# Moving two additions per chunk of a feed-forward block to GpSimd, and one rounding to VectorE

## The chip, the cores and the metric

The kernel runs on one core of a Trainium2 chip. The metric is the device time of one execution in microseconds. The kernel before was timed three times: 3913.15 us in the median, 3912.57 to 3914.15.

## The reference

The input `x` holds 16 images of 24 channels and 56 by 56 pixels in float32. It goes through four layers. Each layer is a mixer (attention in windows, a state-space scan, a four-direction scan, a row LSTM) and then a feed-forward block, both with a residual addition:

```
x = x + mixer(_ln_c(x))              # normalised over the 24 channels
t = _to_tokens(x)
t = t + ffn(_ln_t(t), W1, b1, W2, b2)
x = _from_tokens(t, x)

def ffn(x, W1, b1, W2, b2):          # q_mul rounds to 5 exponent and 2 mantissa bits, q_acc to 5 and 10
    h = relu(_qlinear(x, W1, b1))    # 24 -> 96
    return _qlinear(h, W2, b2)       # 96 -> 24
```

`_qlinear(x, W, b)` is `q_acc(q_acc(q_mul(x) @ q_mul(W).T) + q_mul(b))`. The first format is held as float8 (e5m2), the second as float16.

## The kernel before

`x` lies in SBUF through the whole program as 128 lanes by 4 times 3136 columns: four groups of images at lanes 0, 32, 64 and 96 with 24 lanes each. A mixer writes its result to `mixed` in DRAM, and `feed_forward_phase` follows it, four times in all (layer 0 to 3). That function is what the change touches.

It cuts the 12544 columns into 32 chunks of N = 392. For chunk c it does this:

- SyncE loads the mixer's result of the chunk into one of four buffers (`load`, L220, four transfers, one for each lane group), up to six chunks ahead.
- `add_mixed`: VectorE adds it to `x` (L308).
- `subtract_mean`: TensorE multiplies the chunk by a centring matrix in float32 (L418) into the PSUM bank `xc_ff`.
- `square` (ScalarE, L362), `variance` (TensorE, L425, a product with an averaging matrix), then Ln and Exp on ScalarE (L368, L372), which give the inverse deviation.
- `quantize`: VectorE multiplies the centred bank by it and rounds to float8 (L285).
- `hidden_units`: TensorE makes the 96 hidden units of the four groups in two halves (L436). ScalarE rounds each half to float16 (`round_hidden`, L379), VectorE adds the bias and rectifies (`rectify`, L292), and then rounds all to float8 (`quantize_hidden`, L303).
- `second_product`: TensorE, four products into the bank `ps_y` (L449).
- `round_result`: ScalarE rounds that to float16 (L386). `add_bias` (L321) and `update` (L314) on VectorE add the bias and then the sum to `x`.
- In the layers 0 to 2 the updated chunk is normalised for the next mixer: `subtract_mean` into the bank `xc_ln`, square, `variance` into `ps_y`, Ln, Exp, and `norm` on VectorE (L330), which SyncE stores (L237). In the last layer SyncE stores the chunk of `x` itself (L231).

The chunks are pipelined by an order that is written out by hand. The function `slots` calls a body `slot(s)` on each engine for s = 0 to 34. In slot s an engine works on chunk s+1 (the centring for it), s (inverse deviation, `quantize`), s-1 (hidden units), s-2 (second product, result) and s-3 (norm). The order within slot s is:

- VectorE: `quantize(s)`, `add_mixed(s+1)`, first half of `rectify(s-1)`, `add_bias(s-2)`, `update(s-2)`, second half of `rectify(s-1)`, `quantize_hidden(s-1)`, `norm(s-3)`.
- ScalarE: Ln and Exp of s, first half of `round_hidden(s-1)`, `round_result(s-2)`, the square for the norm of s-3, second half of `round_hidden(s-1)`, square of s+1, Ln and Exp for the norm.
- TensorE: both halves of `hidden_units(s-1)`, `second_product(s-2)`, centring for the norm of s-3, centring of s+1, variance for the norm, variance of s+1.

Every engine runs its instructions in the order written, and semaphores count the finished ones (`added`, `centred`, `quantized`, `biased`, `updated` and so on). GpSimd has no work in this function.

Of the kernel before, what the change touches and what calls it, by code (L numbers as in the profile page):

```python
# [12 lines left out]
ALU = mybir.AluOpType  # L13
# [112 lines left out]
AHEAD = 6  # L126


def feed_forward_phase(nc, x, mixed_dram, normed_dram, out_dram, w, st, layer, by_image=False):
# [6 lines left out]
    with ExitStack() as ctx:  # L136
# [37 lines left out]
        ff, ln = st.ff, st.ln  # L174

        all_loads = (layer + 1) * 6 * 16
        preps = 12
# [24 lines left out]
        with nc.Block() as block:  # L202
            @block.sync
            def _(sp):

                sp.dma_start(centre[:], w["centre"]).then_inc(st.weights_in, 16)
                sp.dma_start(average[:], w["average"]).then_inc(st.weights_in, 16)
                sp.dma_start(w1f[:], w["ff_w1"][layer]).then_inc(st.weights_in, 16)
                sp.dma_start(w2f[:], w["ff_w2"][layer]).then_inc(st.weights_in, 16)
                sp.dma_start(b1f[:], w["ff_b1"][layer]).then_inc(st.weights_in, 16)  # L210
                sp.dma_start(b2f[:], w["ff_b2"][layer]).then_inc(st.weights_in, 16)

                def load(j, k, b):
# [3 lines left out]
                    for g in range(G):  # L217
                        rows = (mixed_dram[j + g * J, :, k * N:(k + 1) * N] if by_image
                                else mixed_dram[c + g * CHUNKS])
                        sp.dma_start(group_rows(mixed[b], g), rows  # L220
                                     ).then_inc(st.mixed_in[b], 16)

# [18 lines left out]
                sp.wait_ge(st.prepared, prep0 + 1)  # L241
                for k in range(AHEAD):
# [14 lines left out]
            def _(dve):  # L257

                for b in range(UNROLL):
# [14 lines left out]
                dve.wait_ge(st.prepared, prep0 + 11)  # L274
# [4 lines left out]
                def quantize(c):  # L279
# [5 lines left out]
                    dve.tensor_tensor(xq[:], xc["ff"][:, 0:N], rstd["ff"][:], ALU.mult,  # L285
# [19 lines left out]
                def add_mixed(c, turn, u):  # L305

                    dve.wait_ge(st.mixed_in[u], (turn + (layer * (CHUNKS // UNROLL) + 1)) * G * 16)
                    dve.tensor_tensor(x[:, bass.ds(c * N, N)], x[:, bass.ds(c * N, N)],  # L308
                                      mixed[u][:], ALU.add).then_inc(ff["added"], 1)

                def update(c):

                    dve.wait_ge(ff["biased"], c + 1 + fb)
                    dve.tensor_tensor(x[:, bass.ds(c * N, N)], x[:, bass.ds(c * N, N)],  # L314
                                       yb[:], ALU.add).then_inc(ff["updated"], 1)
# [36 lines left out]
                add_mixed(0, 0, 0)  # L352
                slots(dve, slot)

            @block.scalar
            def _(act):
# [3 lines left out]
                def square(s, name, base, c):  # L360
                    act.wait_ge(s["centred"], c + 1 + base)
                    act.activation(squares[name][:], xc[name][:, 0:N], ACT.Square  # L362
# [19 lines left out]
                def round_result(c):  # L382

                    act.wait_ge(ff["summed"], c + 1 + fb)
                    reached(act, ff["biased"], c + fb)
                    act.activation(y16[:], ps_y[:, 0:N], ACT.Copy).then_inc(ff["summed16"], 1)  # L386

                def slot(s, turn, u, on):
# [4 lines left out]
                    if on[2]:  # L393
                        round_result(s - 2)
                    if not last and on[3]:
                        square(ln, "ln", nb, s - 3)
                    if on[1]:
                        round_hidden(s - 1, 1)
                    if has_next(s):
                        square(ff, "ff", fb, s + 1)  # L400
# [3 lines left out]
                square(ff, "ff", fb, 0)  # L404
# [4 lines left out]
            def _(pe):  # L409
                pe.wait_ge(st.weights_in, all_loads)  # L410
# [1934 lines left out]
```

## Time and profile before

| quantity | value |
|---|---|
| median of three runs | 3913.15 us |
| the profiled execution | 3912.36 us |
| its span in the trace | 3910.5 us |
| TensorE busy | 3205.9 us, 82% |
| VectorE busy | 2733.1 us, 70% |
| ScalarE busy | 2623.9 us, 67% |
| GpSimd busy | 1638.0 us, 42% |
| mean granted TensorE clock | 0.943 of full speed |

The busy times are sums over the whole program, and the four feed-forward stages are four stretches in it, which begin at 822.8, 2391.5, 3134.5 and 3719.5 us of the trace; the last ends with the program. GpSimd has no instruction in these stretches. The granted clock says what share of full speed (2.4 GHz) TensorE had; it is either 1 or 0.5 at any moment, and a number between is a mean.

### The profile page before, as it was taken

Reading aid. Unit: us, or ns where it says so; the run is one execution under the profiler, and the core shown is the slowest. Engines: PE = TensorE matmul, PEld = TensorE weight load, DVE = VectorE, ACT = ScalarE, POOL = GpSimd, SP = SyncE. Lnnn points to the kernel's source line nnn. Section 1 sums busy time; section 2 is a strip of 40 time slices with the busy share of each in tenths; the row PEclk is TensorE's granted clock in tenths of the full one; section 3 lists DMA queues with packets and bytes.
Section 4 is the critical chain, followed back from the end, with each engine's and each line's share of the span. In section 5 each row is a group of like instructions: output and inputs, shape, how many; then the busy total and the mean of one; then the engine's idle time right before and its main releaser. Section 6 shows DMA issues by size and latency. Waiting matters only on the chain. (4 is left out here: it accounts for less than half of the span.)

```text
span 3910.5 us, 70731 instructions
## 1 busy us (share of the span) xinstructions
PE 3205.9 (82%) x20680; PEld 1815.2 (46%) x20680; DVE 2733.1 (70%) x4347; ACT 2623.9 (67%) x4852; POOL 1638.0 (42%) x1502
## 2 busy tenths in 40 slices
PE   5799999978678898999999666878888678677666
PEld 2688888844224343444444222433343334566522
DVE  2566666657319998999999992749999867122256
ACT  4455555559698888989889434966666378465556
POOL 0233333310147888989889761007677600000000
PEclk9899999989889999999999997989999889798988
DMA  4100000012365747576674522210000022400022
GB/s 95 28 14 14 14 14 14 14 32 60 86 165 161 193 134 197 141 209 172 175 204 120 135 58 68 59 36 20 21 21 20 12 50 54 87 13 13 17 56 51
DMA packets 209512, 297.93 MB, mean 76 GB/s; under 512 B 73866, under 2 KB 193854, under 8 KB 208962
## 3 DMA queue, kind: packets, MB, share of 16 engines
q1 hardware_dynamic: 198546, 285.75, 28.2%
q10 hardware_dynamic: 10800, 10.34, 1.1%
q8 instruction: 58, 0.95, 0.1%
q14 instruction: 108, 0.88, 0.1%
HBM read 193.87 MB, written 102.03 MB: 76 GB/s over the span
## 5 line engine op out<-in xcount | busy, mean ns | idle before, releaser
L1586 POOL TENSOR_TENSOR mam_hc<-mam_h,mam_cs 128x896 f32<-128x896 f32 x336 | 704.0, 2096 | 181.4 <-DVE mam_h L1551 93.3
L1551 DVE TENSOR_TENSOR_SCAN mam_h<-mam_a,mam_kept,mam_dbx 128x448 f32<-128x448 f32 x672 | 737.5, 1127 | 19.9 <-ACT mam_a L1437 18.5
L1318 PE MATMUL mam_ps_y<-mam_hc,mam_ident 128*128 128x448 f32 x1344 | 569.7, 557 | 132.5 <-POOL mam_hc L1586 132.2
L1987 POOL TENSOR_TENSOR scan_ch<-scan_h,scan_cs 128x392 f32<-128x392 f32 x256 | 342.6, 1357 | 394.4 <-DVE scan_h L1931 317.3
L1437 ACT ACTIVATE mam_a<-mam_ft,mam_a_neg 128x448 f32<-128x448 f32 x672 | 409.3, 657 | 79.5 <-DVE mam_h L1551 78.7
L1318 PEld LDWEIGHTS mam_ps_y<-mam_hc,mam_ident 128*128 128x128 f32 x1344 | 248.5, 192 | 431.8 <-POOL mam_hc L1586 222.7
L1538 DVE TENSOR_TENSOR mam_dbx<-mam_ps_u,mam_bs 128x448 f32<-128x448 f32 x672 | 380.8, 610 | 34.2 <-DMA mam_bs<-dram_bc 34.2
L766 POOL TENSOR_TENSOR att_prob<-att_prob,att_share 128x588 f32<-128x588 f32 x128 | 151.6, 1184 | 452.5 <-DVE att_share L951 452.5
L2107 PE MATMUL lstm_ps<-lstm_hs,lstm_w_h 64*128 64x224 f32 x1344 | 175.8, 417 | 97.0 <-DVE lstm_hs L2190 97.0
L418 PE MATMUL f_xc_ff<-all_x,f_centre 128*128 (+1 forms) x256 | 127.8, 583 | 138.8 <-DVE all_x L308 138.7
L886 ACT ACTIVATE att_pt<-att_ps_t 128x512 f32<-128x512 f32 x128 | 76.4, 597 | 210.2 <-PE att_ps_t L827 210.2
L379 ACT ACTIVATE f_h<-f_hid 96x784 f16<-96x784 f32 x256 | 206.8, 810 | 0.0
L1819 PE MATMUL scan_ps_merged<-scan_ch,scan_w_merge 64*128 64x392 f32 x1024 | 202.6, 530 | 3.9 <-POOL scan_ch L1987 3.5
L2107 PEld LDWEIGHTS lstm_ps<-lstm_hs,lstm_w_h 64*128 64x128 f32 x1344 | 149.1, 222 | 120.9 <-DVE lstm_hs L2190 116.3
L867 ACT ACTIVATE att_keys<-att_ps_keys 24x392 f32<-24x392 f32 x384 | 186.5, 486 | 22.4 <-PE att_ps_keys L795 19.4
L1807 PE MATMUL scan_ps_in<-scan_xin,scan_w_in 128*128 128x392 f32 x512 | 187.5, 510 | 6.8 <-ACT scan_rest L1880 4.9
L837 PE MATMUL att_ps_out<-att_pt,att_vals 128*24 128x49 f32 x2048 | 189.5, 208 | 2.1 <-ACT att_pt L886 2.1
L839 PE MATMUL att_ps_out<-att_pt,att_vals 128*24 128x49 f32 x2048 | 187.3, 207 | 0.0
L803 PEld LDWEIGHTS att_ps_vals<-att_nvals,att_xw 128*64 128x64 f32 x4096 | 130.5, 138 | 75.5 <-issue 75.5
L2177 DVE TENSOR_TENSOR lstm_added<-lstm_gates,lstm_new 128x224 f32<-128x224 f32 x56 | 21.9, 392 | 204.7 <-ACT lstm_gates L2137 204.7
L957 DVE TENSOR_SCALAR att_result<-att_ps_out,att_b_out 24x392 f32<-24x392 f32 x128 | 78.6, 614 | 116.4 <-PE att_ps_out L839 116.4
L1931 DVE TENSOR_TENSOR_SCAN scan_h<-scan_decay_by_column,scan_h,scan_drive_by_column 128x392 f32<-128x392 f32 x112 | 158.8, 1418 | 0.2
(214 smaller groups left out, 7464.4 us busy)
## 6 DMA issues: line engine op xcount, KB each, us to landing
mam_taps<-normed SPq DMA_DIRECT2D x1008, 43.5 KB
mam_bs<-dram_bc SPq DMA_DIRECT2D x28, 896.0 KB, 14.3
mam_cs<-dram_bc SPq DMA_DIRECT2D x28, 896.0 KB, 16.6
mam_ft<-dram_steps SPq DMA_DIRECT2D x42, 448.0 KB, 4.8
normed<-f_staged SPq DMA_DIRECT2D x384, 38.1 KB
f_mixed<-mixed SPq DMA_DIRECT2D x384, 36.8 KB
dram_gs<-mam_gs SPq DMA_DIRECT2D x56, 224.0 KB, 2.1
mam_gt<-dram_gs SPq DMA_DIRECT2D x56, 224.0 KB, 2.7
```

What stands on the lines that cost most here:

```text
L379: act.activation(h16[:, 2 * a:2 * a + 2, :], hid[a][0:HID, :, 0:N], ACT.Copy).then_inc(ff["hidden16"], 1)
L837: pe.matmul(ps_out[0:C, cols], vals[p][:, win, 0:C], pt[p][:, q, 64 * half:64 * half + T], start=True, stop=False)
L839: mm = pe.matmul(ps_out[0:C, cols], vals[p][:, win, C:2 * C], pt2[p][:, q, 64 * half:64 * half + T], start=False, stop=True)
L1318: mm = pe.matmul(ps_y[p % 2][:, 0:MT], ident[:], hc[t % 2][:, i, :], start=False, stop=(t % 8 == 7 and i == 1))
L1437: act.activation(a[t % 3][:, i, :], ft[p % 2][:, 0, :], ACT.Exp, scale=a_neg[:, at:at + 1]).then_inc(decays, 1)
L1538: dve.tensor_tensor(dbx[:, i, 0:MT], ps_u[:, 0:MT], bs[:, 2 * pair + i, :], ALU.mult).then_inc(driven, 1)
L1551: dve.tensor_tensor_scan(h[:, n % 8, :], a[t % 3][:, i, :], dbx[:, i, 0:MT], kept[:, at:at + 1], ALU.mult, ALU.add).then_inc(scanned, 1)
L1586: pool.tensor_tensor(hc[t % 2][:], h[:, row:row + 2, :], cs[:, 2 * pair:2 * pair + 2, :], ALU.mult).then_inc(weighed, 1)
L1807: pe.matmul(ps_in[i][:, 0:N], w_in[:, i, :], xin[p][:, :, 1:SIDE + 1], start=True, stop=True).then_inc(projected, 1)
L1819: mm = pe.matmul(ps[:, 0:N], w_merge[rows, n, :], ch[rows, n, :], start=(n == 0), stop=(n == DIRS - 1))
L1987: pool.tensor_tensor(out, hd, in_order(cs, 1 - half, d, k), ALU.mult).then_inc(weighed, 1)
L2107: mm = pe.matmul(ps[p][:, pair, half, 0:W], w_h[lanes, tap, pair, :], hs[lanes, :, y, tap:tap + SIDE], start=False, stop=(tap == 2))
```

## The change

- `add_mixed` and `update` leave VectorE and go to GpSimd. GpSimd first adds the chunks 0, 1 and 2 (`AHEAD_ADDED = 3`), and then for c = 0 to 31 it does `update(c)` and `add_mixed(c + 3)`. Its instructions are written out without a loop.
- `round_result` leaves ScalarE and goes to VectorE, ahead of `add_bias`.
- In the last layer the centred chunk alternates between the banks `xc_ff` and `xc_ln` (`fronts`), and `subtract_mean` waits for the `quantize` of one chunk earlier than before.
- GpSimd clears a tile of squares, and TensorE multiplies it by itself three times into `ps_y` (`WARM_UP = 3`) before it waits for the weights.
- The first buffer is cleared by itself, and the load of chunk 0 is issued behind the two matrices and ahead of the four transfers of the layer's weights. TensorE waits for the prepared weights only after the front of chunk 0.

```diff
+AHEAD_ADDED = 3
+WARM_UP = 3
+        fronts = (xc["ff"], xc["ln"]) if last else (xc["ff"], xc["ff"])
 @block.sync
                 sp.dma_start(centre[:], w["centre"]).then_inc(st.weights_in, 16)
                 sp.dma_start(average[:], w["average"]).then_inc(st.weights_in, 16)
+                sp.wait_ge(st.prepared, prep0 + 1)
+                load(0, 0, 0)
                 sp.dma_start(w1f[:], w["ff_w1"][layer]).then_inc(st.weights_in, 16)
                 ...
-                for k in range(AHEAD):
+                for k in range(1, AHEAD):
 @block.vector
                 def slot(s, turn, u, on):
                     if on[0]:
-                        quantize(s)
-                    if has_next(s):
-                        add_mixed(s + 1, turn + int(u == UNROLL - 1), (u + 1) % UNROLL)
+                        quantize(s, u)
                     if on[1]:
                         rectify(s - 1, 0)
                     if on[2]:
+                        round_result(s - 2)
                         add_bias(s - 2)
-                        update(s - 2)
                     if on[1]:
                         rectify(s - 1, 1)
                         quantize_hidden(s - 1, (u - 1) % 2)
+                def round_result(c):
+                    dve.wait_ge(ff["summed"], c + 1 + fb)
+                    dve.tensor_copy(y16[:], ps_y[:, 0:N]).then_inc(ff["summed16"], 1)
+            @block.gpsimd
+            def _(pool):
+                pool.memset(squares["ln"][:], 0.0).then_inc(warm, 1)
+                def add_mixed(c):
+                    pool.wait_ge(st.mixed_in[c % UNROLL],
+                                 (c // UNROLL + (layer * (CHUNKS // UNROLL) + 1)) * G * 16)
+                    pool.tensor_tensor(x[:, c * N:(c + 1) * N], x[:, c * N:(c + 1) * N],
+                                       mixed[c % UNROLL][:], ALU.add).then_inc(ff["added"], 1)
+                def update(c):
+                    pool.wait_ge(ff["biased"], c + 1 + fb)
+                    pool.tensor_tensor(x[:, c * N:(c + 1) * N], x[:, c * N:(c + 1) * N],
+                                       yb[:], ALU.add).then_inc(ff["updated"], 1)
+                for c in range(AHEAD_ADDED):
+                    add_mixed(c)
+                for c in range(CHUNKS):
+                    update(c)
+                    if c + AHEAD_ADDED < CHUNKS:
+                        add_mixed(c + AHEAD_ADDED)
 @block.scalar
                 def slot(s, turn, u, on):
-                    if on[2]:
-                        round_result(s - 2)
 @block.tensor
+                pe.wait_ge(warm, 1)
+                for _ in range(WARM_UP):
+                    pe.matmul(ps_y[:, 0:N], squares["ln"][:, 0:P], squares["ln"][:], start=True,
+                              stop=True)
                 pe.wait_ge(st.weights_in, all_loads)
-                pe.wait_ge(st.prepared, prep0 + preps)
                 ...
-                    reached(pe, s[reader], c + base)
-                    pe.matmul(xc[name][:, 0:N], centre[:], x[:, bass.ds(c * N, N)],
+                    held = int(last)
+                    if base > 0 or not isinstance(c, int) or c > held:
+                        pe.wait_ge(s[reader], c + base - held)
+                    to = fronts[u % 2] if name == "ff" else xc[name]
+                    pe.matmul(to[:, 0:N], centre[:], x[:, bass.ds(c * N, N)],
                 front(0)
+                pe.wait_ge(st.prepared, prep0 + preps)
```

## Rows read from the trace of the kernel before

**Rows 1.** Windows; after the stretch: length, busy by engine, clock, DMA share, GB/s

```profile
856.00:1000.00 144.00, 127.31 (x529) 62.30 (x528) 111.30 (x275) 132.80 (x250) 0.00 (x0) 1.00 0.24 57
3747.00:3900.00 153.00, 104.74 (x440) 48.42 (x439) 102.38 (x264) 100.38 (x176) 0.00 (x0) 0.93 0.23 55
830.00:848.00 18.00, 12.45 (x27) 4.71 (x26) 3.85 (x12) 6.82 (x12) 0.00 (x0) 0.50 0.15 33
```

**Rows 2.** Line 285 in each feed-forward stage from slot 2: min/median/max ns, first and last start

```profile
L285 DVE TENSOR_TENSOR f_xq<-f_xc_ff,f_rstd_ff x30: 560/566/568, 847.9 to 999.0; 128x392 fp8e5<-128x392 f32 x30
...
L285 DVE TENSOR_TENSOR f_xq<-f_xc_ff,f_rstd_ff x30: 560/566/567, 2416.8 to 2569.1; 128x392 fp8e5<-128x392 f32 x30
...
L285 DVE TENSOR_TENSOR f_xq<-f_xc_ff,f_rstd_ff x30: 560/566/567, 3158.6 to 3310.4; 128x392 fp8e5<-128x392 f32 x30
...
L285 DVE TENSOR_TENSOR f_xq<-f_xc_ff,f_rstd_ff x30: 559/566/568, 3744.8 to 3896.8; 128x392 fp8e5<-128x392 f32 x30
```

**Rows 3.** Timeline, last stage, one slot: start us, duration us, engine, line, idle before

```profile
3782.45 0.57 DVE L285 TENSOR_TENSOR f_xq<-f_xc_ff,f_rstd_ff 128x392 fp8e5<-128x392 f32 x1
3782.93 0.56 DVE L308 TENSOR_TENSOR all_x<-all_x,f_mixed 128x392 f32 x1
...
3783.64 0.92 PE L418 MATMUL f_xc_ff<-all_x,f_centre 128*128 x2 [1.09 <-DVE all_x L308]
...
3784.60 0.50 ACT L362 ACTIVATE f_squares_ff<-f_xc_ff 128x392 f32<-128x392 f32 x1 [0.51 <-PE f_xc_ff L418]
...
3785.24 0.90 PE L425 MATMUL f_var_ff<-f_squares_ff,f_average 128*128 128x392 f32 x2 [0.68 <-ACT f_squares_ff L362]
...
3786.17 0.59 ACT L368 ACTIVATE f_logvar_ff<-f_var_ff,f_eps_t 128x392 f32<-128x392 f32 x1 [1.08 <-PE f_var_ff L425]
...
3787.48 0.57 DVE L285 TENSOR_TENSOR f_xq<-f_xc_ff,f_rstd_ff 128x392 fp8e5<-128x392 f32 x1
```

**Rows 4.** Timeline, first stage, one slot

```profile
858.14 0.80 ACT L379 ACTIVATE f_h<-f_hid 96x784 f16<-96x784 f32 x1
...
858.39 0.57 DVE L285 TENSOR_TENSOR f_xq<-f_xc_ff,f_rstd_ff 128x392 fp8e5<-128x392 f32 x1
...
859.35 0.41 DVE L292 TENSOR_SCALAR f_hr<-f_h,f_b 96x784 f16<-96x784 f16 x1
...
859.57 0.92 PE L418 MATMUL f_xc_ff<-all_x,f_centre 128*128 x2 [0.49 <-DVE all_x L308]
...
859.69 0.31 DVE L321 TENSOR_SCALAR f_yb<-f_y,f_b 128x392 f16<-128x392 f16 x1
...
863.53 0.57 DVE L285 TENSOR_TENSOR f_xq<-f_xc_ff,f_rstd_ff 128x392 fp8e5<-128x392 f32 x1
```

**Rows 5.** Two products on GpSimd, by line: min/median/max ns, first and last start

```profile
L1987 POOL TENSOR_TENSOR scan_ch<-scan_h,scan_cs x256: 1007/1217/1870, 2638.0 to 3123.1; 128x392 f32<-128x392 f32 x128
...
L1620 POOL TENSOR_TENSOR mam_yi<-mam_yi,mam_gt x56: 1122/1140/1535, 1401.6 to 2386.2; 128x448 f32<-128x448 f32 x56
```

**Rows 6.** Groups by form, VectorE: busy us, mean ns, idle before it

```profile
L303 DVE CAST f_h<-f_hr 96x1568 fp8e5<-96x1568 f16 x128 | 123.9, 968 | 5.4
...
L957 DVE TENSOR_SCALAR att_result<-att_ps_out,att_b_out 24x392 f32<-24x392 f32 x128 | 78.6, 614 | 116.4 <-PE att_ps_out L839 116.4
```

**Rows 7.** A VectorE product beside GpSimd's in the second mixer, by line

```profile
L1527 DVE TENSOR_TENSOR mam_ps_u<-mam_ft x42: 595/1171/2198, 1155.4 to 2311.0; 128x448 f32<-128x448 f32 x42
```

**Rows 8.** Timeline, first stage, slot 1, granted clock 0.5

```profile
842.25 1.67 PE L418 MATMUL f_xc_ff<-all_x,f_centre 128*128 128x392 f32 x2 [1.23 <-DVE all_x L308]
...
847.86 0.56 DVE L285 TENSOR_TENSOR f_xq<-f_xc_ff,f_rstd_ff 128x392 fp8e5<-128x392 f32 x1
```

**Rows 9.** Timeline, set-up of the first stage

```profile
825.52 11.53 SPq L220 DMA_DIRECT2D f_mixed<-mixed  x24
...
827.38 0.36 DVE L270 CAST f_w<-f_w1f 128x384 fp8e5<-128x384 f32 x1 [1.97 <-DMA f_b2f<-in_ff_b]
...
829.27 1.65 PE L418 MATMUL f_xc_ff<-all_x,f_centre 128*128 128x392 f32 x2 [9.28 <-DVE all_x L308]
```

More of the change, by code:

```diff
@@ L174, in feed_forward_phase @@
         ff, ln = st.ff, st.ln
+        warm = buf.sem("warm")
+        fronts = (xc["ff"], xc["ln"]) if last else (xc["ff"], xc["ff"])
         all_loads = (layer + 1) * 6 * 16
-        preps = 12
+        preps = 13
         prep0 = layer * preps
@@ L204, in _ @@
             def _(sp):
[L206 to L211, printed above, removed]
                 def load(j, k, b):
@@ L257, in _ @@
             def _(dve):
-                for b in range(UNROLL):
+                dve.memset(mixed[0][:], 0.0).then_inc(st.prepared, 1)
+                for b in range(1, UNROLL):
                     cleared = dve.memset(mixed[b][:], 0.0)
@@ L277, in _, with quantize @@
                 dve.wait_ge(st.prepared, prep0 + preps)
-                def quantize(c):
+                def quantize(c, u):
                     dve.wait_ge(ff["scaled"], c + 1 + fb)
@@ L303, in quantize_hidden @@
                     dve.tensor_copy(h8[p][:], hr[:], saturate=False).then_inc(ff["hidden8"], 1)
[L305 to L315, printed above, removed]
+                def round_result(c):
+                    dve.wait_ge(ff["summed"], c + 1 + fb)
+                    dve.tensor_copy(y16[:], ps_y[:, 0:N]).then_inc(ff["summed16"], 1)
                 def add_bias(c):
@@ L358, in _, with square @@
                 act.wait_ge(st.prepared, prep0 + preps)
-                def square(s, name, base, c):
+                def square(s, name, base, c, u):
                     act.wait_ge(s["centred"], c + 1 + base)
-                    act.activation(squares[name][:], xc[name][:, 0:N], ACT.Square
+                    from_ = fronts[u % 2] if name == "ff" else xc[name]
+                    act.activation(squares[name][:], from_[:, 0:N], ACT.Square
                                    ).then_inc(s["squared"], 1)
@@ L392, in slot @@
                         round_hidden(s - 1, 0)
-                    if on[2]:
-                        round_result(s - 2)
                     if not last and on[3]:
-                        square(ln, "ln", nb, s - 3)
+                        square(ln, "ln", nb, s - 3, u)
                     if on[1]:
@@ L399, in slot @@
                     if has_next(s):
-                        square(ff, "ff", fb, s + 1)
+                        square(ff, "ff", fb, s + 1, u + 1)
                     if not last and on[3]:
                         inverse_deviation(ln, "ln", nb, eps_c, "normed", s - lag)
-                square(ff, "ff", fb, 0)
+                square(ff, "ff", fb, 0, 0)
                 slots(act, slot)
@@ L453, in front @@
                 def front(c):
-                    subtract_mean(ff, "ff", fb, "added", "quantized", c)
+                    subtract_mean(ff, "ff", fb, "added", "quantized", c, c)
                     variance(ff, "ff", fb, c)
@@ L463, in slot @@
                     if not last and on[3]:
-                        subtract_mean(ln, "ln", nb, "updated", "normed", s - 3)
+                        subtract_mean(ln, "ln", nb, "updated", "normed", s - 3, u)
                     if has_next(s):
-                        subtract_mean(ff, "ff", fb, "added", "quantized", s + 1)
+                        subtract_mean(ff, "ff", fb, "added", "quantized", s + 1, u + 1)
                     if not last and on[3]:
```

19 lines of the change are left out of this document (10 added, 9 removed).

## The prediction

> **What bounds the kernel now.** The table of windows comes first. In the steady part of the first feed-forward stage ScalarE is busy 132.80 of 144.00 us and TensorE 127.31, GpSimd nothing; in the last stage TensorE is busy 104.74, VectorE 102.38 and ScalarE 100.38 of 153.00 us [rows 1]. No engine is full there, so an order of work sets the pace, not an engine's load. The grouped line of `quantize` then gives that pace. There is one `quantize` in a slot, and from slot 2 to slot 31 there are 29 intervals in 151.1, 152.3, 151.8 and 152.0 us, 607.2 us in all or 5.23 us for each of the 116 [rows 2]. Last, the timeline shows the ring that makes it. In the last stage, `quantize` starts at 3782.45, `add_mixed` 0.48 us later, the centring product at 3783.64 (its idle time ends by that addition), the square at 3784.60, the variance at 3785.24, Ln at 3786.17 and the next `quantize` at 3787.48: 0.48 + 0.71 + 3.84 = 5.03 us [rows 3]. In the first stage the part from centring to `quantize` is 863.53 - 859.57 = 3.96 us [rows 4], and the slot 5.14 us. So in every stage the centring of chunk s+1 waits for an addition that stands behind `quantize(s)` on VectorE. Only the way from `quantize(s)` to that centring is 1.18 us long, and this is where the change works.
>
> **What the new queues do to this ring.** GpSimd runs `update(c)` and then `add_mixed(c + 3)`. Put c = s-2: the addition that the centring of chunk s+1 needs is `add_mixed(s+1)`, and it stands right behind `update(s-2)`. `update(s-2)` waits for `add_bias(s-2)`, and that stands on VectorE behind `quantize(s)`, half of `rectify(s-1)` and the new `round_result(s-2)`. Being three chunks ahead is thus no lead at all: the third chunk is the one that is wanted in the same slot. The ring stays one slot long and gets longer. From `quantize(s)` at 0, in the first stage:
>
> - ScalarE's first half of `round_hidden` ends at 858.14 + 0.80 = 858.94, 0.55 after `quantize` at 858.39 [rows 4]. `rectify` can start at 0.60 (I take 0.05 to 0.06 for a hand-over). What follows it starts 859.69 - 859.35 = 0.34 later, at 0.94.
> - `round_result` on VectorE, 128x392 from PSUM, isn't in the trace. Above it lies the 0.61 of a VectorE operation on 392 float32 from PSUM [rows 6], below it the 0.31 of `add_bias` on float16 in SBUF [rows 4]. I take 0.57, what `quantize` needs, for that reads the same number from PSUM [rows 3]. It ends at 1.51.
> - `add_bias` starts at 1.57 and takes 0.31 [rows 4]: 1.88. GpSimd starts `update` at 1.94.
> - A GpSimd product of two 128x392 float32 tiles takes 1.007 at least and 1.217 in the median [rows 5]. An addition, one with a float16 operand, isn't shown; I take 1.01 for each of the two: 2.95 and 3.96. Another 0.09 to TensorE: 4.05.
> - From centring to `quantize` as before, 3.96 in the first three stages and 3.84 in the last.
>
> That gives 8.01 and 7.89 us for a slot, if TensorE keeps its full clock and nobody disturbs GpSimd: 116 intervals take 87 x 8.01 + 29 x 7.89 = 926 us, 319 us more than now.
>
> **Two things come on top.** First, collisions between VectorE and GpSimd. A VectorE product of 448 columns takes 595 ns at its shortest and 1171 in the median, up to 2198, while GpSimd is at work in that mixer; GpSimd's of 448 go from 1.12 to 1.54 us there [rows 5, 7]. So one collision costs GpSimd about 0.41 us. Whether the forms used here collide isn't shown. While GpSimd does its two additions, VectorE has the second half of `rectify` (0.41) and the float8 rounding (0.97 [rows 6]) to do. The price lies between 0 and 0.41 + 0.97 = 1.38 us a slot; I take 0.4, the price of the collision that rows 5 show.
>
> The Trainium skill ("SBUF — State Buffer", section "Who interferes with whom") says that VectorE and GpSimd share a pair of ports as an exclusive lock, that a VectorE cast or tensor_scalar in a two-port mode takes it, and that the later of the two waits for the whole other instruction. By that rule an addition could wait for both `rectify` and the rounding, 1.38 us a slot, 160 us in 116 slots; rows 7 agree with a lock, because 2198 is 595 plus most of a long GpSimd instruction, but they don't show these forms.
>
> Second, TensorE's clock. With a slot of 8.4 us TensorE's work per slot, now 127.31 / 144.00 x 5.14 = 4.5 us, becomes 54% of the time, and in the last stage 104.74 / 153.00 x 5.1 = 3.5 us, 42%, with about 3 us in one piece in which it waits for GpSimd. At 88% busy the granted clock is 1.00, at 68% it is 0.93, and it was 0.50 in the stretch behind the idle set-up, though TensorE was busy 69% of it at that slow pace [rows 1]. So I expect it to fall in many slots and to come back behind the dense part. At half clock, centring to `quantize` took 847.86 - 842.25 = 5.61 us instead of 3.96 [rows 8]; from the same rows I estimate that the second product, for which `round_result` waits, would be late by 0.5, and that the variance for the norm adds 0.25, since each of these products takes nearly twice as long (1.67 for 0.92). That's 1.65 + 0.75 = 2.4 us a slot at most. I take half, 1.2, since nothing shows how often the clock falls; the ends are 0 and 2.4.
>
> **The small parts.** The first two intervals of a stage lose the 0.5 us of `add_mixed` (three chunks are already added): 4 x 2 x 0.5 = -4 us. At a stage's end the last `update` takes 1.01 us on GpSimd, where an addition on VectorE takes 0.56 [rows 3]: +0.5 x 4 = +2. Set-up: one transfer takes 11.53 / 24 = 0.48 us to issue, so the weights come 4 x 0.48 = 1.9 us later, and they were in at 827.38: 829.3. TensorE still waits for all six before the front of chunk 0, which now starts at 829.27 [rows 9]. I count 0, bounds -1 to +2 a stage. The products of zeros end some 2 us before these weights are in. At best they would keep the clock for the first three chunks, 3 x 1.65 = 5 us a stage; I count 0. The second bank in the last stage takes away the wait for `quantize(s)`, which isn't the last to end any more: 0, as the addition comes 3 us after it; gained if the addition were early. What ScalarE is spared in a slot lay beside the ring, and costs or gains 0. Loads: one for chunk c+6 is issued behind the store of chunk c, as before, and now has the longer slots to land in: 0.
>
> **Sum.** A slot is 8.0 + 0.4 + 1.2 = 9.6 us, in the last stage 9.5: 87 x 9.6 + 29 x 9.5 = 1110.7 us instead of 607.2, so +503.5. With -4 and +2 it is +501.5 on the profiled execution's 3912.36 us (span 3910.5; 0.8 below the median of the three runs): 4414 us, which I round to 4415.
>
> **The rivals.**
> - *GpSimd is fully locked out* (the rule above): another 1.38 - 0.4 = 1.0 us a slot, 116 us, 4530 us. For it speaks the 2198 ns of rows 7. Against it: one of the two additions can start ahead of the VectorE operation, which then waits instead and off this ring.
> - *The bare ring*: clock full, no collision, +317: 4230 us. For it speaks only that the clock was 0.93 at 68% busy.
> - *Not slower*: GpSimd's additions are ready before `quantize(s)` ends, so the centring starts right behind it and the slot is 0.57 + 0.06 + 3.96 = 4.6 us. 116 x 0.63 = 73 us less, 3840 us. The place is the end of `add_mixed(s+1)`; it decides as soon as that lies before 0.6 us in the slot. It can't unless `update(s-2)` comes before `quantize(s)`, and the order on VectorE says otherwise. Only if I misread that order does this happen.
> - *Nothing changes*: the longer way is hidden. The ring has no slack: its parts add up to the slot [rows 3].
>
> **How the numbers follow.** The forecast gets 0.78, full lock 0.12, the bare ring 0.06, not slower 0.03, nothing changes 0.01. The range goes from the bare ring, 4230, to 4640: half clock all the time and full lock would be 8.0 + 1.4 + 2.4 = 11.8 us a slot and 4670, which I hold for too rare to take in whole. A measurement of this kernel can tell 0.2%, about 8 us, from no change. Faster by more: 0.03. Within: 0.01. Slower: 0.96.
>
> **What would show it.** In the profile after, `quantize` should come every 8 to 10 us, and TensorE's centring should wait for GpSimd's `all_x` in nearly every slot, as the largest wait of the stage. `update` and `add_mixed` should stand back to back on GpSimd, 1.0 us each or longer where `rectify` or the rounding overlap. The granted clock in the stages should be between 0.6 and 0.9. ScalarE's busy share of the first stage should fall from 92% to about half. The prediction is wrong if the centring waits for `quantize` or not at all, if `add_mixed(s+1)` runs before `update(s-2)`, or if a slot is under 7.5 us; an addition of 0.6 us on GpSimd would take 0.8 off the slot.

## The result, and the profile after

The changed kernel takes 4416.4 us in the median of four runs (4413.4 to 4418.9), the kernel before 3913.7 beside it: 1.128 times as long, with a 95% interval of 1.127 to 1.130. The profiled execution took 4413.4 us with a span of 4412.0. The forecast was 4415.

The windows of the steady part of the first and of the last feed-forward stage answer to [rows 1]: length, then busy time of PE, PEld, DVE, ACT and POOL, granted clock, DMA share, GB/s.

```profile
860.00:1120.00 260.00, 170.95 (x523) 84.06 (x523) 129.58 (x248) 127.24 (x222) 59.34 (x56) 0.80 0.13 31
4120.00:4380.00 260.00, 141.47 (x381) 60.83 (x379) 94.00 (x208) 77.23 (x128) 70.21 (x52) 0.67 0.12 29
```

TensorE is busy 66% and 54% of these stretches, at a granted clock of 0.80 and 0.67 where it had 1.00 and 0.93. ScalarE fell from 92% to 49%. Every engine that worked here before has a smaller share of the time than it had, so the engines wait more.

The grouped line of `quantize` answers to [rows 2]: the first stage, then the last, where the two banks make two lines.

```profile
L292 DVE TENSOR_TENSOR f_xq<-f_xc_ff,f_rstd_ff x30: 560/566/568, 847.5 to 1120.9; 128x392 fp8e5<-128x392 f32 x30
...
L292 DVE TENSOR_TENSOR f_xq<-f_xc_ff,f_rstd_ff x15: 560/561/561, 4099.7 to 4386.4; 128x392 fp8e5<-128x392 f32 x15
L292 DVE TENSOR_TENSOR f_xq<-f_xc_ln,f_rstd_ff x15: 560/561/567, 4110.1 to 4396.7; 128x392 fp8e5<-128x392 f32 x15
```

A slot is (1120.9 - 847.5) / 29 = 9.43 us in the first stage and (4396.7 - 4099.7) / 29 = 10.24 in the last; the second and third stage have 9.38 and 9.40. The 116 intervals take 1114.9 us instead of 607.2.

By line, what waits for `add_mixed` (L360), and the other pieces of the ring with min/median/max in ns: `update` (L366), `round_result` (L315), the float8 rounding (L310) and `rectify` (L299).

```profile
L360 POOL TENSOR_TENSOR all_x<-all_x,f_mixed x128: 1006/1128/1738, 827.3 to 4389.3; 128x392 f32<-128x392 f32 x128
...
who waited for it (us, times):
  PE f_xc_ff L438: 332.8, 101
  PE f_xc_ln L438: 59.5, 15
...
L366 POOL TENSOR_TENSOR all_x<-all_x,f_yb x128: 922/924/1152, 849.7 to 4407.5; 128x392 f32<-128x392 f32 x128
...
L315 DVE CAST f_y<-f_ps_y x128: 552/555/567, 848.7 to 4406.5; 128x392 f16<-128x392 f32 x128
...
L310 DVE CAST f_h<-f_hr x128: 967/1572/1658, 842.7 to 4403.3; 96x1568 fp8e5<-96x1568 f16 x128
...
L299 DVE TENSOR_SCALAR f_hr<-f_h,f_b x256: 409/419/1269, 841.7 to 4402.9; 96x784 f16<-96x784 f16 x128
```

In 101 + 15 = 116 chunks TensorE's centring waits for GpSimd's `add_mixed`, 392 us in all. The float8 rounding, 0.97 us before, now takes 1.57 in the median, `rectify` up to 1.27: these are collisions, as the two timelines below show.

The timeline of one slot of the last stage answers to [rows 3]. It begins with the centring of the chunk whose `quantize` follows.

```profile
4196.67 1.67 PE L438 MATMUL f_xc_ff<-all_x,f_centre 128*128 x2 [4.01 <-POOL all_x L360]
4198.37 0.50 ACT L384 ACTIVATE f_squares_ff<-f_xc_ff 128x392 f32<-128x392 f32 x1 [5.36 <-PE f_xc_ff L438]
...
4199.02 1.64 PE L445 MATMUL f_var_ff<-f_squares_ff,f_average 128*128 128x392 f32 x2 [0.68 <-ACT f_squares_ff L384]
...
4202.17 0.56 DVE L292 TENSOR_TENSOR f_xq<-f_xc_ff,f_rstd_ff 128x392 fp8e5<-128x392 f32 x1 [6.52 <-ACT f_rstd_ff L394]
...
4202.65 0.41 DVE L299 TENSOR_SCALAR f_hr<-f_h,f_b 96x784 f16<-96x784 f16 x1
4202.98 0.57 DVE L315 CAST f_y<-f_ps_y 128x392 f16<-128x392 f32 x1
4203.58 0.32 DVE L321 TENSOR_SCALAR f_yb<-f_y,f_b 128x392 f16<-128x392 f16 x1
4203.82 0.41 DVE L299 TENSOR_SCALAR f_hr<-f_h,f_b 96x784 f16<-96x784 f16 x1
4203.98 1.03 POOL L366 TENSOR_TENSOR all_x<-all_x,f_yb 128x392 f32<-128x392 f32 x1 [7.46 <-DVE f_yb L321]
4204.27 1.57 DVE L310 CAST f_h<-f_hr 96x1568 fp8e5<-96x1568 f16 x1
...
4204.98 1.74 POOL L360 TENSOR_TENSOR all_x<-all_x,f_mixed 128x392 f32<-128x392 f32 x1
...
4206.86 1.01 PE L438 MATMUL f_xc_ln<-all_x,f_centre 128*128 x1 [3.92 <-POOL all_x L360]
```

The whole ring is here: 5.50 us from centring to `quantize` (both products at half clock, 1.67 and 1.64 us), then 4.69 us through `rectify`, `round_result`, `add_bias`, `update` and `add_mixed` to the next centring. Two more things stand in it. The rounding L310 begins inside `update`, which ends at 4205.01, and is through at 4205.84, 0.60 later than alone. `add_mixed` begins at 4204.98 and takes 1.74 instead of 1.01: it ends 0.88 behind the rounding. Each waited for the other in turn.

The mean clock of 0.67 hides where the two levels lie. Two windows of this slot, in the same columns as above, first while TensorE works and then while it waits for `add_mixed`:

```profile
4196.60:4202.20 5.60, 4.86 (x12) 2.19 (x13) 0.03 (x2) 1.97 (x4) 0.00 (x0) 0.50 0.18 41
4202.30:4205.60 3.30, 0.64 (x4) 0.17 (x2) 3.22 (x7) 0.96 (x2) 1.62 (x2) 1.00 0.00 0
```

TensorE has half clock while it works and the full one while it mostly waits. The clock is at half again (0.50) from 4205.8 us, before the wait ends at 4206.86. In the last stage the part from the end of `add_mixed` to the next `quantize` therefore takes 5.65 us in the mean.

A slot of the first stage answers to [rows 4]. The slots there are not alike (8.3 to 10.5 us); this one shows the collision that is usual in them.

```profile
886.67 0.57 DVE L292 TENSOR_TENSOR f_xq<-f_xc_ff,f_rstd_ff 128x392 fp8e5<-128x392 f32 x1
887.25 0.42 DVE L299 TENSOR_SCALAR f_hr<-f_h,f_b 96x784 f16<-96x784 f16 x1
...
887.59 0.55 DVE L315 CAST f_y<-f_ps_y 128x392 f16<-128x392 f32 x1
...
888.18 0.32 DVE L321 TENSOR_SCALAR f_yb<-f_y,f_b 128x392 f16<-128x392 f16 x1
888.58 0.92 POOL L366 TENSOR_TENSOR all_x<-all_x,f_yb 128x392 f32<-128x392 f32 x1 [7.41 <-DVE f_yb L321]
888.63 1.09 DVE L299 TENSOR_SCALAR f_hr<-f_h,f_b 96x784 f16<-96x784 f16 x1
889.46 1.13 POOL L360 TENSOR_TENSOR all_x<-all_x,f_mixed 128x392 f32<-128x392 f32 x1
889.76 1.66 DVE L310 CAST f_h<-f_hr 96x1568 fp8e5<-96x1568 f16 x1
890.73 1.09 PE L438 MATMUL f_xc_ff<-all_x,f_centre 128*128 x2 [3.37 <-POOL all_x L360]
```

Here `rectify` comes just behind `update`'s start and pays (1.09 for 0.41), so that GpSimd goes on almost undisturbed, and the rounding pays too (1.66). In the mean of this stage `update` takes 0.95 and `add_mixed` 1.23 us, in the last stage 1.03 and 1.74. The same collision lies on the ring in one stage and mostly off it in the other, by who comes first: in the last stage ScalarE has no square of the norm to do, its second half of `round_hidden` is ready sooner, and `rectify` starts ahead of `update`.

### The profile page after: what moved, and what is told of

Its sections match the earlier page's. It is cut to its first block and busy times, and to the rows that moved or that the text cites. A ratio compares the mean times of both kernels' runs of the same rounds, so it can differ in the third digit from the quotient of the medians.

```text
span 4412.0 us, 70463 instructions
## 1 busy us (share of the span) xinstructions
PE 3420.1 (78%) x20704; PEld 1914.9 (43%) x20704; DVE 2787.4 (63%) x4219; ACT 2588.0 (59%) x4724; POOL 1924.9 (44%) x1762
## 5 line engine op out<-in xcount | busy, mean ns | idle before, releaser
L366 POOL TENSOR_TENSOR all_x<-all_x,f_yb 128x392 f32<-128x392 f32 x128 | 124.0, 969 | 932.3 <-DVE f_yb L321 932.3
L438 PE MATMUL f_xc_ff<-all_x,f_centre 128*128 (+1 forms) x224 | 156.7, 795 | 349.8 <-POOL all_x L360 332.8
L384 ACT ACTIVATE f_squares_ff<-f_xc_ff 128x392 f32<-128x392 f32 x112 | 55.7, 497 | 406.9 <-PE f_xc_ff L438 386.9
L330 DVE TENSOR_TENSOR f_staged<-f_xc_ln,f_rstd_ln 128x392 f32<-128x392 f32 x96 | 54.5, 568 | 302.0 <-ACT f_rstd_ln L394 301.7
L438 PEld LDWEIGHTS f_xc_ff<-all_x,f_centre 128*128 128x128 f32 x224 | 46.3, 257 | 420.2 <-issue 393.5
L445 PE MATMUL f_var_ff<-f_squares_ff,f_average 128*128 128x392 f32 x256 | 181.2, 805 | 31.3 <-ACT f_squares_ff L384 31.1
L310 DVE CAST f_h<-f_hr 96x1568 fp8e5<-96x1568 f16 x128 | 189.7, 1482 | 5.4
```

The costliest lines, as they stand in the source:

```text
L310: dve.tensor_copy(h8[p][:], hr[:], saturate=False).then_inc(ff["hidden8"], 1)
L438: pe.matmul(to[:, 0:N], centre[:], x[:, bass.ds(c * N, N)], start=True, stop=True).then_inc(s["centred"], 1)
L445: pe.matmul(var[name][:, 0:N], average[:], squares[name][:], start=True, stop=True).then_inc(s["varied"], 1)
```

## The experiments

All times are medians, and each ratio is to the kernel before on the same chip. The kernel before took 3913.8 us beside e1 to e4, 3915.8 beside e5, e6, e8 and e9, and 3908.4 beside e10 to e12, so times of different groups are compared by their ratios. The indented text ahead of each result is what was expected before the run. The code cuts are shortened. "Slot" is the mean of the 29 intervals of `quantize` from slot 2, in the first and in the last stage; the mixers between the stages vary by some 10 us from run to run, so a small effect is better read from the slots than from the time.

| run | time us | ratio to before (95%) | slot, first stage | slot, last stage |
|---|---|---|---|---|
| before | 3913.2 | 1 | 5.21 | 5.24 |
| changed | 4416.4 | 1.128 (1.127 to 1.130) | 9.43 | 10.24 |
| e1_ahead4 | 3868.6 | 0.989 (0.987 to 0.992) | 5.18 | 4.35 |
| e2_round_scalar | 4315.7 | 1.103 (1.101 to 1.104) | 8.52 | 9.83 |
| e3_update_vector | 3867.2 | 0.987 (0.986 to 0.989) | 5.14 | 4.30 |
| e4_filled_gap | 4292.3 | 1.096 (1.094 to 1.098) | 8.37 | 9.21 |
| e5_no_rounding | 4386.2 | 1.120 (1.116 to 1.123) | 9.28 | 9.91 |
| e12_filled_no_rounding | 4246.3 | 1.086 (1.085 to 1.088) | 8.16 | 8.35 |
| e6_ahead4_no_warm | 3881.4 | 0.990 (0.987 to 0.994) | 5.21 | 4.36 |
| e8_ahead4_loads7 | 3879.2 | 0.990 (0.987 to 0.993) | 5.25 | 4.35 |
| e9_ahead4_one_bank | 3889.9 | 0.993 (0.990 to 0.995) | 5.10 | 4.68 |
| e10_update_vector_loads7 | 3863.0 | 0.988 (0.986 to 0.990) | 5.06 | 4.33 |
| e11_update_vector_loads7_round_scalar | 3848.6 | 0.984 (0.983 to 0.986) | 4.84 | 4.46 |

**Is it the order on GpSimd, or its load?** The first run differs from the changed kernel in one figure.

```diff
-AHEAD_ADDED = 3
+AHEAD_ADDED = 4
```

> GpSimd adds four chunks at first instead of three, so the addition of chunk s+1 stands ahead of the update of chunk s-2 instead of behind it. Nothing else differs from the changed kernel. Ring theory: the centring of s+1 then only waits for its bank (0.57 + 0.06 + 3.96 = 4.6 us) or for ScalarE's and VectorE's own work, so a slot falls from 9.4 and 10.2 us to 4.6 to 5.2 us, TensorE's clock is back at 0.95 or more in the stages, and the time is 3830 to 3890 us, 530 us less than the changed kernel and below the kernel before. Rival, GpSimd's load: two additions a slot on GpSimd and their collisions with VectorE are what is slow, whatever the order. Then a slot stays above 8 us and the time above 4250 us.

```profile
856.00:1000.00 144.00, 131.14 (x534) 59.81 (x533) 124.84 (x253) 126.18 (x225) 55.05 (x56) 1.00 0.24 58
```

```profile
L360 POOL TENSOR_TENSOR all_x<-all_x,f_mixed x128: 1007/1014/1746, 827.1 to 3844.9; 128x392 f32<-128x392 f32 x128
its engine sat idle before it (us, times) until:
  DMA f_mixed<-mixed: 125.8, 64
  DMA f_mixed<-by_image: 56.9, 30
```

Both GpSimd additions are still there in every slot, 55 us in 144, and some still collide (1746 ns at most), but 548 us are gone: 3868.6, as the ring theory had it; only the last stage's 4.35 us a slot is shorter than its 4.6, since with two banks the centring doesn't wait for `quantize`. The rival of GpSimd's load falls. What made the kernel slow was that `add_mixed(s+1)` stood behind `update(s-2)` of the same slot. It is also 1.1% (0.8 to 1.3%) faster than the kernel before.

The second run leaves the order of the additions alone and cuts the ring elsewhere.

```diff
 pool:  for c in range(CHUNKS):
-           update(c); add_mixed(c + AHEAD_ADDED)
+           add_mixed(c)
 vector, slot:  add_bias(s - 2)
+               update(s - 2)
```

> The changed kernel with update back on VectorE, while add_mixed stays on GpSimd and runs as far ahead as the loads let it. Ring theory: no addition that the centring waits for stands behind anything of the same slot, so the ring is cut as well: a slot of 4.6 to 5.2 us, 3830 to 3900 us. Rival, collisions with GpSimd: one of two GpSimd operations is left, so half of the loss stays, 4100 to 4200 us.

3867.2 us, where the rival had 4100 to 4200. Two different cuts of the same ring give the same time, so it was the ring.

**How long is `round_result` in the ring?** It goes back to ScalarE, in its old place of the slot.

```diff
 scalar, slot:  round_hidden(s - 1, 0)
+               round_result(s - 2)
 vector, slot:
-               round_result(s - 2)
                add_bias(s - 2)
```

> The changed kernel with round_result back on ScalarE, as before the change. Ring theory: the rounding on VectorE is 0.57 us of the ring. On ScalarE it runs beside half of rectify and ends 0.94 us behind quantize, so the update starts 0.5 us earlier in each of 116 slots: 60 us less, 4330 to 4370 us, the rest of the ring unchanged. Rival (the rounding isn't on the path, because GpSimd or the clock sets the slot): within 10 us of 4412.

```profile
860.00:1080.00 220.00, 148.26 (x495) 73.25 (x495) 103.73 (x211) 128.68 (x235) 51.95 (x53) 0.84 0.15 36
4030.00:4280.00 250.00, 153.53 (x387) 63.34 (x385) 93.94 (x178) 90.37 (x154) 50.22 (x50) 0.55 0.13 30
```

4315.7 us, 101 less than the changed kernel and below my range. The rounding's own part was right: the shortest slots of the first stage are 7.4 us where those of the ring at full clock are 7.9 to 8.1 in e12_filled_no_rounding. What I left out is what such a shift sets off. In the last stage `update` and `add_mixed` now take 0.92 and 1.13 us, against 1.03 and 1.74 in the changed kernel: GpSimd is hardly held up any more. The collision is still there, but VectorE pays for it, with 1.66 us for the rounding and 0.63 for `rectify` in the mean. So 0.55 + 0.72 us could have been gained, and only 0.41 is seen. The granted clock fell from 0.67 to 0.55 there, and the second product, at half clock, now ends 1.15 us behind the start of `quantize` instead of 0.77. `update` waits for that product by way of `round_result` and `add_bias`, and starts 2.17 us behind `quantize` instead of 1.86. In the first stage the clock rose from 0.80 to 0.84, and 0.91 is seen.

**What does the clock cost?** TensorE multiplies in the gap. The products are overwritten.

```diff
+FILL = 12
-                    if ready is not None:
-                        pe.wait_ge(ff[ready], c + 1 + fb)
                     ...
                     to = fronts[u % 2] if name == "ff" else xc[name]
+                    if ready == "added" and (not isinstance(c, int) or c > 3):
+                        for _ in range(FILL):
+                            pe.matmul(to[:, 0:P], centre[:], centre[:], start=True, stop=True)
+                    if ready is not None:
+                        pe.wait_ge(ff[ready], c + 1 + fb)
```

> The changed kernel, but TensorE runs 12 products of the centring matrix by itself (128 columns each) into the bank of the centring, ahead of its wait for GpSimd's addition. The results are overwritten. They take some 2.6 us of the 3 to 4 us gap. Clock theory: the fall of the granted clock in this gap costs 1.2 to 1.6 us a slot. With the gap filled the granted clock is 0.97 or more in the stages and a slot falls to the bare ring of 8.0 to 8.2 us in the first three stages and about 8.6 in the last (where the addition collides with VectorE's rounding by 0.73): 4412 - 87 x 1.3 - 29 x 1.6 = 4250 us, between 4225 and 4280. Rival: the products that run at half clock lie beside the ring. Then the time stays at 4412 us or rises, since the fillers can delay the centring.

```profile
860.00:1080.00 220.00, 200.14 (x1149) 134.25 (x1148) 129.39 (x237) 120.23 (x213) 59.06 (x54) 1.00 0.15 36
4020.00:4260.00 240.00, 183.04 (x1023) 128.56 (x1022) 96.50 (x212) 80.01 (x132) 71.16 (x52) 0.87 0.13 32
```

The granted clock is 1.00 in the first stage, and the slot falls by 1.06 us, with twelve more products in it. In the last stage it reaches only 0.87, and the slot falls by 1.03. With 4292.3 us the run is 12 above my range, because I had left the collisions out of the first three stages and the rest of the clock's loss out of the last. The rival had 4412 us or more and falls, so that the clock costs time is shown: 124 us of 503 come back. That is a lower bound of its part. The last stage still isn't at full clock, and `quantize` to the end of `add_mixed` grew by 0.1 to 0.2 us a slot in this run, while the rest of the slot, where TensorE's products lie, fell by 1.14 us in the first three stages and by 1.25 in the last.

**What do the collisions cost?** The rounding of the hidden units is left out, and its two tiles are cleared once in each stage.

```diff
+                for p in range(2):
+                    dve.memset(h8[p][:], 0.0)
                     ...
-                    dve.tensor_copy(h8[p][:], hr[:], saturate=False).then_inc(ff["hidden8"], 1)
+                    dve.memset(gate[:, 2:3], 0.0).then_inc(ff["hidden8"], 1)
```

> The changed kernel without the rounding of the hidden units to float8 on VectorE (quantize_hidden writes one column elsewhere; the second product takes zeros). It leaves that part of the computation out, to see what its collision with GpSimd's add_mixed costs. In the changed kernel's last stage add_mixed takes 1.74 us in every slot, against 1.01 alone. Lock theory: without the rounding it takes 1.01 there, the slot of the last stage falls by 0.7 us from 10.2, that of the first three by the 0.3 us that some slots with 1.74 make in the mean: 29 x 0.7 + 87 x 0.3 = 46 us, 4365 us, between 4340 and 4390. Rival: add_mixed is slow for another reason, and the rounding lies beside the ring: 4412 us, within 10.

```profile
L362 POOL TENSOR_TENSOR all_x<-all_x,f_mixed x128: 1002/1010/1221, 826.8 to 4365.7; 128x392 f32<-128x392 f32 x128
```

A slot of the last stage, where L294 is `quantize` and L317 `round_result`:

```profile
4203.51 1.46 PE L471 MATMUL f_ps_y<-f_h,f_w 96*128 96x392 fp8e5 x4
4203.69 0.56 DVE L294 TENSOR_TENSOR f_xq<-f_xc_ff,f_rstd_ff 128x392 fp8e5<-128x392 f32 x1 [7.28 <-ACT f_rstd_ff L396]
...
4205.01 0.57 DVE L317 CAST f_y<-f_ps_y 128x392 f16<-128x392 f32 x1 [0.43 <-PE f_ps_y L471]
```

`add_mixed` is at 1.01 us in the median and never above 1.22, where it reached 1.74. That the rounding held it up is shown. But the time fell by 30 us instead of 46, and the slot of the last stage by 0.33 instead of 0.73: the clock fell once more, to 0.55 in that stage. The lines show where it tells: the second product takes 1.46 us at half clock, and `round_result` waits 0.43 us for it, which it doesn't in the slot of the changed kernel above. `update` starts 2.28 us behind `quantize` instead of 1.86, and that is the 0.4 us that is missing. So both were taken away together.

> The changed kernel with TensorE's gap filled (as in e4_filled_gap) and without the float8 rounding of the hidden units (as in e5_no_rounding, which leaves that part of the computation out). Theory: clock and collision both come on top of a ring of 8.0 us, and e5_no_rounding gained only 28 us instead of 46 because the clock fell further in the last stage (0.57 instead of 0.67). With both away every slot is 7.9 to 8.1 us, in the last stage 7.8 to 8.4: 4240 us, between 4220 and 4260. Rival: the collision costs nothing by itself; then it is at e4_filled_gap's 4292 us.

```profile
860.00:1080.00 220.00, 204.96 (x1173) 137.24 (x1172) 91.58 (x246) 122.84 (x217) 54.40 (x54) 1.00 0.15 37
4010.00:4230.00 220.00, 175.44 (x1034) 123.28 (x1032) 57.84 (x214) 79.56 (x132) 54.09 (x54) 0.91 0.15 35
```

4246.3 us, with all slots of the first stage from the third of the 29 intervals on between 7.91 and 8.12 us. That's the length of the prediction's bare ring (8.01). The rounding's collision is worth 0.21 us a slot in the first stage and 0.86 in the last once the clock no longer gives it back. `rectify` still collides in this run (0.69 us in the mean of the first stage), so this isn't the price of all collisions.

The slots of these runs can be cut in two at the end of `add_mixed`: what stands ahead of it is the work of VectorE and GpSimd, with the wait for the second product, and what stands behind it is the way from the centring to the next `quantize`, with TensorE's two products. Means over the 29 intervals in us:

| run | three stages: to the end of `add_mixed` | from there to `quantize` | last stage: to the end of `add_mixed` | from there to `quantize` |
|---|---|---|---|---|
| bare ring of the prediction | 3.96 | 4.05 | 3.96 | 3.93 |
| changed | 4.05 | 5.35 | 4.59 | 5.65 |
| e2_round_scalar | 3.52 | 4.93 | 4.18 | 5.65 |
| e4_filled_gap | 4.15 | 4.21 | 4.81 | 4.40 |
| e5_no_rounding | 3.94 | 5.28 | 4.28 | 5.63 |
| e12_filled_no_rounding | 3.97 | 4.20 | 4.03 | 4.31 |

**What do the small parts do?** They were tried on e1_ahead4, where nothing covers them. First the products of zeros (`WARM_UP = 0`):

> e1_ahead4 without the products of zeros ahead of the first chunk. My prediction counted them as nothing, since TensorE waits some 2 us for the weights behind them. If that holds, 3868 us, within 4. Rival: they raise the granted clock in the last stage, whose first two intervals of quantize are 2.9 and 4.0 us instead of 6.7 each before the change; without them the time is 4 to 10 us more.

The trace of the changed kernel shows them in the first stage:

```profile
823.74 4.29 PE L426 MATMUL f_ps_y<-f_squares_ln 128*128 128x392 f32 x6 [3.15 <-POOL f_squares_ln L354]
...
829.58 0.36 DVE L277 CAST f_w<-f_w1f 128x384 fp8e5<-128x384 f32 x1 [3.57 <-DMA f_b2f<-in_ff_b]
829.60 1.68 PE L438 MATMUL f_xc_ff<-all_x,f_centre 128*128 128x392 f32 x2 [1.58 <-DMA f_b2f<-in_ff_b]
```

They end 1.58 us before the weights are in, and the centring takes 1.68 us, at half clock. Without them the first two intervals of the last stage are 4.3 and 4.7 us instead of 2.9 and 4.0, together 2.2 us; in the other stages they are the same within 0.1. But e8_ahead4_loads7, which has the products, has 4.3 and 3.6 us there, and e10_update_vector_loads7, which has them too, 3.9 and 5.1, as much as without them. The time, 3881.4 (3869.9 to 3884.4), can't tell more, because the intervals of the ratios 0.990 and 0.989 overlap. Their worth stays open between 0 and some 2 us.

Then the second bank of the last stage (`fronts = (xc["ff"], xc["ff"])`, `held = 0`):

> e1_ahead4 with one centred bank in the last stage, as before the change. Its slot in the last stage is 4.35 us with two banks. With one bank the centring waits for quantize: 0.57 + 0.06 + 3.84 = 4.5 us. If that ring is all that the second bank takes away, 29 x 0.15 = 4 us more, 3872 us. Rival: the second bank gives more, since the centring can then run while VectorE is busy with a rounding that collides: 4.8 us or more in the slot, over 13 us more.

4.68 us a slot instead of 4.35, and 6.7 and 6.3 us for the first two intervals instead of 2.9 and 4.0: 9.6 + 6.1 = 16 us that the second bank gives once the ring is cut, more than the 4 I had expected, since I took the steady slot alone and its ring 0.18 too short. The 6.1 are uncertain: in the other runs with two banks these two intervals add up to 6.8 to 9.0 us. In the changed kernel, where the centring waits for `add_mixed` 3 us later, the second bank can give only those first intervals; that wasn't run.

**Can the rest be made faster?** e1_ahead4 has GpSimd waiting for loads, 183 us in all. So they come earlier (`AHEAD = 7`):

> Four chunks added at first (as in e1_ahead4), and SyncE loads seven chunks ahead instead of six. In e1_ahead4 GpSimd waited for loads for 183 us, and a slot of the first three stages took 5.15 us, though the ring of one bank is 4.6 and the shortest slots were 4.8. Load theory: with the loads a slot earlier the wait goes and a slot is 4.7 to 4.9 us: 87 x 0.35 = 30 us less than e1_ahead4, 3825 to 3850 us. Rival: ScalarE (126 of 144 us busy) and the collisions on VectorE set the 5.15 us: within 6 us of e1_ahead4's 3868.

```profile
L360 POOL TENSOR_TENSOR all_x<-all_x,f_mixed x128: 1007/1136/1752, 826.4 to 3859.9; 128x392 f32<-128x392 f32 x128
...
L310 DVE CAST f_h<-f_hr x128: 967/1662/1670, 841.9 to 3872.0; 96x1568 fp8e5<-96x1568 f16 x128
```

A miss: the slot is 5.25 us, longer than 5.18. GpSimd's wait for loads is gone, but `add_mixed` now follows `update` directly, and the rounding is held up in most slots (1.66 us in the median). Between 870 and 990 us TensorE's weight loads and products for the second product together wait 16.2 us for the rounding, against 1.3 in e1_ahead4. So, as I read the traces, an addition that came late had kept out of VectorE's way. With `update` on VectorE the two additions can't follow each other on GpSimd:

> update on VectorE and add_mixed on GpSimd (as in e3_update_vector), with loads seven chunks ahead. In e3_update_vector the first three stages take 5.13 us a slot; GpSimd's addition waits for its load there and the centring then for it, and e8_ahead4_loads7 showed that with both additions on GpSimd earlier loads only bring collisions (5.25 us). With one addition on GpSimd there is no float8 rounding to collide with twice. Theory, loads: without that wait a slot is 4.8 to 5.0 us, 87 x 0.2 = 20 us less than e3's 3867, 3835 to 3860 us. Rival, collisions on VectorE again: 3867 us or more.

5.06 us a slot instead of 5.14, and 3863.0 us: the loads gave 0.08 us a slot and not the 0.2 I had expected, and the time is 3 us above my range. The ratio, 0.988, doesn't differ from the 0.987 of e3_update_vector.

> As e10_update_vector_loads7, with round_result back on ScalarE. Only add_mixed has left VectorE then. ScalarE's load is that of the kernel before, 132.8 of 144 us or 4.75 us a slot, VectorE's falls by 0.57. If VectorE is what holds e10 up, this is faster by some 5 to 15 us; if ScalarE does (nothing of it was spared then), a slot is 4.9 to 5.1 us and it is slower than e10 by 5 to 15 us. I hold the second for likelier: 3850 to 3870 us.

The same window of e10_update_vector_loads7 and then of this run:

```profile
870.00:990.00 120.00, 113.01 (x453) 50.24 (x454) 102.60 (x239) 104.84 (x190) 23.27 (x23) 1.00 0.25 60
870.00:990.00 120.00, 113.06 (x471) 54.73 (x471) 97.56 (x225) 116.55 (x222) 23.08 (x23) 1.00 0.25 60
```

The side I held for less likely: 4.84 us a slot and 3848.6 us, 0.984 of the kernel before. ScalarE wasn't what held e10 up: it now does more in a shorter slot, and is busy 97% of the time. What held it up was `round_result` on VectorE. It empties the bank `ps_y`, into which the variance for the norm goes, and in this window of e10 TensorE waited 2.9 us for `round_result` ahead of it, and ScalarE 8.3 us for it, here 0.4. Of the change only `add_mixed` on GpSimd, two banks and the new set-up are left in it, and the loads come seven chunks ahead. It is the fastest version I ran. In the last stage, where ScalarE and VectorE have less to do, `round_result` is better off on VectorE (4.33 against 4.46).

## Why the prediction was right, and where not

- *The ring* was read right from the order of the code: `add_mixed(s+1)` behind `update(s-2)` behind `add_bias(s-2)` behind `quantize(s)`. e1_ahead4 moves the one addition and 548 us go; e3_update_vector cuts elsewhere and the same go. The two runs leave no room for GpSimd's load as the cause.
- *Its bare length*, 8.01 and 7.89 us, is measured as 7.91 to 8.12 in the first stage of e12_filled_no_rounding, and as 7.9 in the shortest slots of its last stage. `round_result` was taken as 0.57 and is 0.555. `update` was taken as 1.01 and takes 0.92 undisturbed: the float16 operand costs nothing. `add_mixed` takes 1.01 undisturbed, as taken, but in e12_filled_no_rounding mostly 1.13, because the end of `rectify` still holds it up. These two errors cancel, so that the ring's length came out better than its parts.
- *The collision* was mis-sized, in both directions. I took 0.4 us a slot everywhere. By the difference of e4_filled_gap and e12_filled_no_rounding the rounding's part is 0.2 in the first three stages (8.36 - 8.17 in their mean) and 0.86 in the last (9.21 - 8.35). In the changed kernel itself the part up to the end of `add_mixed` is 0.1 us longer than the bare ring's in the first three stages and 0.6 in the last. The rule of the Trainium skill that I weighed ("SBUF — State Buffer", section "Who interferes with whom") is an exclusive lock in which the later one waits for the whole other instruction. The timelines agree with it to within 0.2 us. In the slot of the last stage the rounding starts 0.74 us ahead of `update`'s end and takes 0.60 longer than alone, and `add_mixed` starts 0.86 ahead of the rounding's end and takes 0.73 longer. In the slot of the first stage `rectify` starts 0.87 ahead of `update`'s end and takes 0.68 longer. The rival's price of 1.38 us a slot wasn't reached, for the reason given with it: each engine loses a turn, and the turn that VectorE loses is off the ring. The last stage should have been priced by itself, for ScalarE's shorter slot puts `rectify` ahead of `update` there.
- *The clock* was taken as 1.2 us a slot, half of what half clock all the time would cost. Filling the gap gives back 1.04 in the first three stages (9.40 - 8.36) and 1.03 in the last (10.24 - 9.21, with the clock at 0.87 and not 1 after the filling). The part of the slot in which the centring and the variance lie says more: it is 1.3 us longer than the bare ring's in the first three stages (5.35 against 4.05) and 1.7 in the last (5.65 against 3.93). So half was about right for three stages and too little for the last, where the clock is at half in the whole of that part. The mechanism holds, as forecast: the clock falls in the wait for GpSimd and comes back behind the dense part.
- *The sum* came within 2 us of the measured time, and that is luck, for its two stages err in opposite directions. The first three stages have 9.40 us a slot and not 9.6, 17 us less than forecast for 87 slots. The last has 10.24 and not 9.5, 21 us more for 29. Together 1114.9 against 1110.7 us.
- *The small parts* came to -7 us (501.0 - 507.7) instead of -2. The first two intervals of the four stages gave -9.5 instead of -4 (42.7 us against 52.2). The largest piece I had not counted: in the last stage they fell from 13.4 to 6.8 us, by the second bank in the main; what else has a part in it isn't shown. The starts and ends of the stages and the mixers make the other +3, and the mixers alone vary by more than that.
- *The rivals.* *Not slower* and *nothing changes* fall with the waits of the 116 chunks for `add_mixed`. *The bare ring*, 4230 us, is what e12_filled_no_rounding comes near with 4246.3: it is right for a kernel without collisions whose clock is held up, and this one isn't that. *Fully locked out*, 4530, falls with the collisions' price: of its 1.38 us a slot only 0.1 to 0.2 are found in three stages, and 0.6 to 0.9 in the last.

## What to carry to other kernels

When work is moved to an engine of its own, write down for one slot what the moved instruction stands behind on its new queue, and what that waits for. "Three chunks ahead" was no lead, because GpSimd ran its instructions in the order written, and the third chunk was wanted in the very slot in which the one before it in the queue became ready; one more chunk turned 12.8% slower into 1.1% faster. And a longer ring costs more than its instructions: here 2.7 to 2.8 us of added work in the slot made 4.2 to 5.0, the rest by the clock that fell in the gap and by the collisions.

## What the runs showed of the hardware

- GpSimd and VectorE shut each other out for nearly the whole of an instruction (all but 0.2 us), in forms that the trace of before didn't have: VectorE's float16 tensor_scalar (0.41 us alone, up to 1.27) and its cast from float16 to float8 (0.97 alone, 1.66) against an addition on GpSimd (1.01 alone, 1.74). Neither engine is starved: where their instructions follow each other closely, each waits in turn.
- A shorter ring can lower the clock. Taking 0.73 us of collision out of the last stage's slot (e5_no_rounding) shortened it by 0.33, while TensorE's clock fell from 0.67 to 0.55 and the second product came 0.4 us later. With the clock held up the same removal gave 0.86. Why the clock fell with the shorter slot isn't shown.
- A mean clock can hide that all the work is done at the low level: in the last stage it is 0.67, but in the slot shown 0.50 while TensorE works and 1.00 while it waits.
- An addition with one float16 operand takes 0.92 us on GpSimd, less than with two float32 operands (1.01).
- A late load can be worth something: with the loads a slot earlier, e8_ahead4_loads7 was slower in the slot (5.25 against 5.18), and the rounding took 1.66 us in the median instead of 0.97 alone.
